# Mixture-of-experts network: the second expert stage scatters its rows to token order, and the last stage loads them as contiguous rows

## The reference

```
x = x + tanh(g_xattn[0]) * attention(norm(x), ctx)         # 16 heads of 64, a bias from side
x = x + tanh(g_ffn[0])   * experts(norm(x))                # 64 experts, best 4, silu, 256 rows each
x = x + tanh(g_xattn[1]) * attention(norm(x), norm(ctx))   # scores clipped to +-11
x = x + tanh(g_ffn[1])   * experts(norm(x))                # 8 experts, best 2, gelu, 1280 rows each
```

## Time and profile before

| | us |
|---|---|
| median of 3 runs | 2124.15 |
| the profiled execution | 2128.7 |
| its span, first to last instruction | 2127.0 |
| experts 1: first instruction to the last row copy's end | 1651.3 to 2035.6 |
| combine: barrier to the end of the span | 2038.0 to 2127.0 |

### The profile page before, as it was taken

How to read it: one execution, slowest core, us unless ns; L and a number is a source line. 1 busy time by engine, 2 the same in 40 slices (tenths; PEclk the granted TensorE clock), 3 DMA queues, 4 the chain that set the end, 5 groups by cost and what they waited for, 6 DMA issues and landing times. The chain is left out here.

```text
span 2127.0 us, 43848 instructions
## 1 busy us (share of the span) xinstructions
PE 1853.9 (87%) x14851; PEld 1671.5 (79%) x14851; DVE 1312.3 (62%) x3630; ACT 997.5 (47%) x2467; POOL 593.7 (28%) x712
## 2 busy tenths in 40 slices
PE   5999999999996599958999999999994699999920
PEld 4888888888885488847888888888883699999920
DVE  2677877877877233336778777878874444444423
ACT  3776677676674133334554454454551333333300
POOL 0012222222232200024243433434312422222056
PEclk9999999999998799978999999999997799999965
DMA  5676011011000599941111111111100422232134
GB/s 196 244 273 241 27 37 37 25 37 36 25 28 24 183 298 298 295 163 46 36 46 46 51 36 44 48 46 43 43 16 30 149 88 88 84 111 67 35 105 147
DMA packets 121821, 205.95 MB, mean 97 GB/s; under 512 B 15856, under 2 KB 63505, under 8 KB 121680
## 3 DMA queue, kind: packets, MB, share of 16 engines
q1 hardware_dynamic: 99408, 145.14, 20.1%
q0 software_dynamic: 22272, 59.05, 8.9%
HBM read 111.56 MB, written 94.37 MB: 97 GB/s over the span
## 5 line engine op out<-in xcount | busy, mean ns | idle before, releaser
L469 POOL DMA_INDIRECT buf<-a_rxn,a_disp x192 | 197.3, 1028 | 253.6 <-DVE comb L853 90.2
L1114 PE MATMUL a_psM<-a_wo,a_oT 128*128 128x256 f32 x1024 | 235.6, 383 | 4.5 <-ACT a_oT L621 1.4
L600 ACT ACTIVATE a_S<-a_S,a_mn 128x128 f32<-128x128 f32 x512 | 199.0, 396 | 68.8 <-DVE a_mn L889 68.8
L1114 PEld LDWEIGHTS a_psM<-a_wo,a_oT 128*128 128x128 f32 x1024 | 192.6, 191 | 36.0 <-issue 3.4
L79 PE MATMUL e_psH<-e_x_hi,e_w_hi 128*128 128x256 f32 x640 | 184.9, 289 | 0.0
L869 DVE TENSOR_TENSOR a_S<-a_S,a_rz 128x512 f32<-128x512 f32 x256 | 177.5, 693 | 8.8
L81 PE MATMUL e_psH<-e_x_hi,e_w_lo 128*128 128x256 f32 x640 | 181.7, 284 | 0.0
L80 PE MATMUL e_psH<-e_x_lo,e_w_hi 128*128 128x256 f32 x640 | 181.6, 284 | 0.0
L79 PE MATMUL a_psP<-a_c_hi,a_wk_hi 128*128 128x256 f32 x512 | 155.4, 303 | 11.1 <-DVE a_c_lo L746 11.1
L79 PE MATMUL a_psP<-a_x_hi,a_wq_hi 128*128 128x256 f32 x512 | 157.5, 308 | 5.2 <-DVE a_x_lo L746 5.2
L1077 PE MATMUL a_psT<-ident,a_S 128*128 128x128 f32 x1024 | 139.3, 275 | 18.7 <-DVE a_S L869 18.7
(11 more groups left out here) (184 smaller groups left out, 4904.6 us busy)
## 6 DMA issues: line engine op xcount, KB each, us to landing
y<-e_y SPq DMA_DIRECT2D x104, 256.0 KB, 2.9
buf<-a_zeros SPq DMA_DIRECT2D x16, 1280.0 KB, 7.0
buf<-a_zeros SPq DMA_DIRECT2D x16, 1024.0 KB, 5.9
e_rows<-buf SPq DMA_DIRECT2D x64, 256.0 KB, 3.9
e_w_in<-in_L_ffn_w SPq DMA_DIRECT2D x64, 256.0 KB, 3.2
a_ctx<-in_ctx SPq DMA_DIRECT2D x32, 256.0 KB, 2.9
e_w_out<-in_L_ffn_w SPq DMA_DIRECT2D x64, 128.0 KB, 3.8
e_w<-in_L_ffn_W_in SPq DMA_DIRECT2D x8, 1024.0 KB, 6.8
```

The lines of the kernel that those rows point to most:

```text
L469: g_.indirect_dma_start(out=buf, out_offset=bass.IndirectOffsetOnAxis(ap=disp[:, par, i, k:k + 1], axis=0), in_=rxn[:, par, i], in_offset= ...
L600: ins = a.activation(s[:, h], s[:, h], ACT.Exp, bias=mn[:, u % 2, h:h + 1], scale=-1.0, accum_out=z[:, u % 2, h:h + 1])
L1114: ins = mm(psM[:, 0], oT[:, c], wo[:, c], start=c == 0, stop=c == HP - 1)
```

## The change

Each row that attention 1 scatters to buf1 now carries its token's number plus one, in 8 added columns (rows of 264 numbers, 1056 bytes, instead of 256). Empty slots read zeros there. Experts 1 adds to this number, per chunk, a value for the slot (`target`): -1 for a first choice, 4095 for a second, 65535 for a slot past the expert's count. The sum is the row of y1, now 2 x 4096 rows in token order; rows past the bound are not written. GpSimd scatters each chunk by two indirect DMAs in place of SyncE's store, 7 chunks behind the gathers. `gates` moves to the end of VectorE's loop and no longer computes slots. y1 is cleared during attention 1 by 32 DMAs of 256 KB, since dropped choices are written by nobody. Combine loads y1 by 16 DMAs of 512 KB from SyncE into one tile for everything (4 token tiles and one choice each), and ScalarE issues the 16 stores. So that there are semaphores enough, those of attention 0 are cleared by GpSimd during experts 0, where it is otherwise idle.

The diff, cut to its core (semaphore renaming and tile allocations are left out):

```
@@ attention, SyncE
-                    for u in range(UG):
-                        sp.wait_ge(s_sc, at(g, WG, u // 2 + 1))
-                        clear(g * UG + u)
-                    load_ctx(g + 3)
+            sp.wait_ge(s_rwz, 2)
+            for g in range(PEEL):
+                for u in range(UG):
+                    sp.wait_ge(s_sc, at(g, WG, u // 2 + 1))
+                    n = g * UG + u
+                    if not first:
+                        clear("y1", s_zero[0], n, K1 * NTOK * D // P // 512 // (4 * UG), 512)
+                    elif n < 2 * UG:
+                        clear("buf0", s_zero[0], n, ROWS0 * D // P // 512 // (2 * UG), 512)
+                    else:
+                        clear("buf1", s_zero[1], n - 2 * UG, ROWS1 // P // (2 * UG), DW)
+                load_ctx(g + 3)
@@ attention, GpSimd
+                g_.memset(zeros[:], 0.0).then_inc(s_rwz, 1)
@@ attention, VectorE
+                if not first:
+                    ins = v_.tensor_copy(rxn[:, par, :, D:RW], tiles(t.token, g)...)
-                    v_.tensor_copy(tiles(t.idf1, g), idf[:])
@@ experts0
+        @block.gpsimd
+        def _(pool):
+            nc.clear_and_free_semaphores(t.done_sems)
@@ experts1, SyncE
-                    sp.wait_ge(s_ye, it * CB + c + 1)
-                    sp.dma_start(yd[...].rearrange("(p i) n -> p i n", p=P), y[:, c % 2]).then_inc(s_st[c % 2], 16)
@@ experts1, VectorE
+                v_.tensor_tensor(into[:, c % RB], rows[:, c % RB, :, D], target[...], ALU.add).then_inc(s_xlo, 1)
...
+                link(v_.tensor_scalar(source[:], source[:], -BIG, BIG - 1.0, ALU.mult, ALU.add))
+                link(v_.scalar_tensor_tensor(out=target[:], in0=second[:]..., scalar=float(NTOK),
+                                             in1=source[:]..., op0=ALU.mult, op1=ALU.add))
...
-            gates()
             for part in range(3):
                 ve.wait_ge(s_whi, part + 1)
                 weights_lo(0, part)
             each(ve, body)
+            gates()
@@ experts1, GpSimd
+            LAG = 7
+            def scatter(it, c):
+                pool.wait_ge(s_ye, it * CB + c + 1)
+                pool.sem_inc(t.s_passed, 1)
+                for i in range(GT):
+                    g_.indirect_dma_start(out=yd, out_offset=bass.IndirectOffsetOnAxis(ap=into[:, c % RB, i:i + 1], axis=0),
+                                          in_=y[:, c % 2, i], in_offset=None, bounds_check=K1 * NTOK - 1, oob_is_err=False
+                                          ).then_inc(s_st[c % 2], 16)
...
-                        pool.wait_ge(s_tx, (c if fresh else it * CB + c) - RB + 1)
+                        pool.wait_ge(s_xlo, (c if fresh else it * CB + c) - RB + 1)
...
+                    if not fresh or c >= LAG:
+                        scatter(*((it, c - LAG) if c >= LAG else (it - 1, CB + c - LAG)))
...
+            for c in range(CB - LAG, CB):
+                scatter(NIT - 1, c)
+            for i in range(2):
+                pool.wait_ge(s_st[i], NCH // 2 * (16 * GT))
@@ combine
-            for g in range(NG):
-                ...
-                for n in range(GT * K1):
-                    nc.gpsimd.indirect_dma_start(out=rows[:, g % 2, n], out_offset=None, in_=d["y1"], ...)
+            for q in range(NQ):
+                for k in range(K1):
+                    tiles = slice(q * QT, (q + 1) * QT)
+                    sp.dma_start(rows[:, k, tiles], src[k][:, tiles]).then_inc(s_row[q], 16)
...
+        @block.scalar
+        def _(act):
+            for g in range(NG):
+                q, i = divmod(g * GT, QT)
+                act.wait_ge(s_acc, QT * K1 * q + QT + i + GT)
+                nc.scalar.dma_start(d["out"][...], t.x[:, g * GT:(g + 1) * GT]).then_inc(s_out, 16)
```

More of the change, by code:

```diff
@@ new lines, in attention @@
+        s_tc = sem(L + "context_transposed")
+        NS = 3
+        s_xT = sem(L + "x_transposes_evacuated")
+        s_cT = sem(L + "context_transposes_evacuated")
+        s_pj = sem(L + "projected")
+        s_ev = [sem(L + f"projection_evacuated{i}") for i in range(2)]
+        s_sc = sem(L + "scores_ready")
+        s_read = sem(L + "scores_read")
+        s_exp = sem(L + "exp_ready")
+        RZ = 1 if first else 2
+        s_rz = sem(L + ("sums_inverted" if first else "sums_then_inverse_ready"))
@@ L243, in attention @@
             rows = m.sb(L + "rows", [P, GT * K0, D])
[L244 to L247, removed]
+            s_ix = sem(L + "indices_copied")
+            s_row = [sem(L + f"rows_gathered{i}") for i in range(2)]
+            s_acc = sem(L + "row_added")
+            s_cn = sem(L + "context_normed")
             cstats = m.sb(L + "cstats", [P, GT, 6])
@@ L251, in attention @@
             crs = m.sb(L + "crs", [P, GT])
-            s_cmv = m.sem(L + "context_stats_then_moments_ready")
-            s_cve = m.sem(L + "context_variance_shifted")
-            s_crs = m.sem(L + "context_rstd_ready")
-        else:
-            zeros = m.sb(L + "zeros", [P, 512])
-            s_min = m.sem(L + "min_ready")
-            s_zero = [m.sem(L + f"buffer_{i}_cleared") for i in range(2)]
+            s_cmv = sem(L + "context_stats_then_moments_ready")
+            s_cve = sem(L + "context_variance_shifted")
+            s_crs = sem(L + "context_rstd_ready")
+        else:
+            s_min = sem(L + "min_ready")
+        zeros = m.sb(L + "zeros", [P, 512])
+        s_zero = [sem(L + f"buffer_{i}_cleared") for i in range(2 if first else 1)]
         NR = 1 if first else 2
@@ L264, in attention @@
         rw = m.sb(L + "rw", [P, DC, EW])
-        rxn = m.sb(L + "rxn", [P, 2, GT, D])
+        RW = D if first else DW
+        rxn = m.sb(L + "rxn", [P, 2, GT, RW])
         rxT = m.sb(L + "rxT", [P, DC, TOK])
@@ L1413, in experts1 @@
         second = m.sb(L + "second", [P, E, NT])
+        moved = m.sb(L + "moved", [P, E, NT])
+        target = m.sb(L + "target", [P, E * NT])
+        into = m.sb(L + "into", [P, RB, GT], I32)
         source = m.sb(L + "source", [P, E, NT])
@@ L1442, in experts1 @@
         s_ye = m.sem(L + "output_evacuated")
-        s_st = [m.sem(L + f"rows_stored{i}") for i in range(2)]
+        s_st = [m.sem(L + f"rows_scattered{i}") for i in range(2)]
         block = stack.enter_context(nc.Block())
@@ L1497, in _ @@
             with sp.Fori(0, NIT - 1) as it:
[L1498 to L1501, removed]
+                body(it)
         RPI = CB // RB
@@ L1623, in split_x @@
                 ve.wait_ge(s_xhi, it * CB + c + 1)
-                v_.tensor_tensor(x_lo[:, c % 2], psX[c % 2][:], x_hi[:, c % 2].bitcast(F32), ALU.subtract
+                v_.tensor_tensor(x_lo[:, c % 2], psX[c % 2][:], x_hi[:, c % 2].bitcast(F32), ALU.subtract)
+                n0 = it * (CB * GT) + c * GT
+                v_.tensor_tensor(into[:, c % RB], rows[:, c % RB, :, D],
+                                 target[:, n0:n0 + GT] if isinstance(it, int) else target[:, bass.ds(n0, GT)], ALU.add
                                  ).then_inc(s_xlo, 1)
@@ L1773, in _ @@
-        @block.sync
-        def _(sp):
-            for g in range(NG):
-                sp.wait_ge(s_acc, GT * K1 * (g + 1))
-                sp.dma_start(d["out"][g * GT:(g + 1) * GT].rearrange("b p d -> p b d"), t.x[:, g * GT:(g + 1) * GT]
-                             ).then_inc(s_out, 16)
-            sp.wait_ge(s_out, 16 * NG)
+            for q in range(NQ):
+                ve.wait_ge(s_row[q], 16 * K1)
+                for k in range(K1):
+                    for i in range(QT):
+                        n = q * QT + i
+                        x = t.x[:, n]
+                        if k:
+                            ve.wait_ge(s_acc, QT * K1 * q + i + 1)
+                        nc.vector.scalar_tensor_tensor(out=x, in0=rows[:, k, n], scalar=t.prob1[:, n, k:k + 1],
+                                                       in1=x, op0=ALU.mult, op1=ALU.add).then_inc(s_acc, 1)
```

168 lines of the change are left out of this document (76 added, 92 removed).

## The result

The changed kernel takes 2071.28 us, the median of 4 runs (2070.71 to 2074.08), beside 2123.6 us of the kernel before on the same chip: a ratio of 0.9756 with a 95% interval from 0.9739 to 0.9773. It is 52 us faster, where 44 was forecast, and lies 0.3 us above the lower end of the range. The profiled execution took 2070.71 us, with a span of 2069.0.

What follows compares the result with a forecast made beforehand. It took TensorE to bound experts 1 and GpSimd's descriptor lists to bound combine. Combine saves 51 us, the seam costs 6.7, a gain of 44: from the median, 2124.15 - 44 = 2080 us, range 2071 to 2092.

Steps and rivals of the forecast that it cites:

- Combine, 38 us forecast: Last stage, from barrier to end: 38 us instead of 89.0, between 34.6 and 41.7, saving 51 us.
- the lower of the two bounds: Combine if loads never hold up VectorE: 4.9 first load + 26.7 adds + 2.6 last store + 0.4 barrier = 34.6 us.
- The sum of transfers: Combine's DMA: 22.8 us loads plus 12.1 us stores, 34.9 us; with latency and the end 37.3 us.
- The seam, 6.7 us forecast: Experts 1 to combine: last scatters, then GpSimd's drain of 6.0 us (3.0 to 9.0), open the barrier 6.7 us later.
- That it grows with the DMAs: Rival at the seam: the drain grows to 13.2 us with 160 DMAs, adding 7.2 us: 2087; chance 0.12.
- GpSimd in experts 1, 6.3 us per chunk forecast: Experts 1: a copy, two gathers and two scatters take GpSimd 6.3 of 9.06 us per chunk, hidden beside TensorE.
- the rival in which VectorE locks GpSimd out: Experts 1: GpSimd stands still through VectorE's work, 10.6 us per chunk, 61 us over 40 chunks: 2141; chance 0.02.
- The clearing in pieces of 1056 bytes: Attention 0: clearing costs by bytes, 59 us within 71, nothing lost; rival of double cost gives 2096, chance 0.06.
- TensorE still fills its window in experts 1 at 9.06 us per chunk: Sign of being right: experts 1 stays bound by TensorE at its earlier pace of 9.06 us per chunk.
- the prediction's own terms for its lower end: Whole kernel: combine at 34.6 instead of 38, drain at 3.0 instead of 6.0, and 2 us left open in attention 1.
- signs of being right: Barrier opens 2041 to 2048 after the drain; add gaps under 2 us, combine 35 to 42; experts 1 9.06 per chunk.
- the signs of being wrong: TensorE idle in experts 1 on x_lo or rows; drain over 10 us; adds waiting throughout combine; attention 0 ending later.

Runs made afterwards that it cites:

- the distance closed: Changed kernel with an unused 704-byte tile ahead of x_hi in experts 1, putting x and h back at the weights' address modulo 1024: 2079.13 us, ratio 0.9784.

## Why the prediction came out as it did

- **Combine, 38 us forecast, 34.2 measured.** The mechanism was right, and the lower of the two bounds (34.6, VectorE's path) was the better one. By pieces: the first add came 5.1 us behind the barrier (4.9 forecast), the adds took 25.42 (26.7 forecast), and 3.7 followed the last add (3.0 forecast). The sum of transfers was too long because they ran faster than the rates from which it was made. The DMA engines of the kernel after, from the barrier to the end, total and by queue:

```profile
DMA packets 6656, 12.58 MB, mean 360 GB/s; under 512 B 512, under 2 KB 4608, under 8 KB 6656
q1 hardware_dynamic: 2304, 8.39, 61.1%
q10 hardware_dynamic: 4352, 4.20, 34.1%
c_rows<-y SPq DMA_DIRECT2D x16, 512.0 KB, 10.1
```

  95% of 35 us for 12.58 MB are 378 GB/s while they run, against 368 and 348 taken from loads and stores apart. That is not a gain of running both at once: the loads alone, from 2038 to 2042 and ahead of the first store's data, moved 409 GB/s, and from 2050 to 2060 loads and stores together 410.
- **The seam, 6.7 us forecast, 7.5 measured.** The drain ended 6.7 us after the last scatter, the mean of four taken was 6.0. That it grows with the DMAs is refuted: 6.7 us after 160 DMAs in the stage, 6.6 after 80. It is 6.6 or 6.7 in all traces that keep the barrier, 2.9 and 8.9 or 9.0 in the attention stages: a fixed length for each place, whose cause stays open. Some 1.4 of the 6.7 us here are GpSimd's own wait for the scatters to land: the drain itself lasts 5.3 us, and where GpSimd does not wait first, in the run without the barrier, it ends 5.3 us after the last scatter.
- **GpSimd in experts 1, 6.3 us per chunk forecast.** Its timeline over one chunk, which answers to the earlier trace rows:

```profile
1881.37 1.01 POOL L1742 DMA_INDIRECT y<-e_y,e_into  x1 [2.17 <-DVE e_y L1663]
1882.69 1.00 POOL L1742 DMA_INDIRECT y<-e_y,e_into  x1 [0.30 <-issue]
1883.67 0.21 POOL L1753 COPY e_cur<-e_source_row 128x2 int32<-128x2 int32 x1
1884.71 1.01 POOL L1757 DMA_INDIRECT e_rows<-buf,e_cur  x1 [0.83 <-POOL e_cur L1753]
1886.03 0.96 POOL L1757 DMA_INDIRECT e_rows<-buf,e_cur  x1 [0.31 <-issue]
1890.20 1.01 POOL L1742 DMA_INDIRECT y<-e_y,e_into  x1 [3.21 <-DVE e_y L1663]
```

  5.6 us of work in 8.83, then a wait for a copy of the result: never the bound. The durations over the stage, scatters and gathers:

```profile
L1742 POOL DMA_INDIRECT y<-e_y,e_into x80: 971/1000/1019, 1687.4 to 2027.0; - x80
L1757 POOL DMA_INDIRECT e_rows<-buf,e_cur x80: 946/976/1930, 1653.9 to 1966.9; - x80
```

  No scatter took over 1.02 us, and the longest gather is as long as before, so the rival in which VectorE locks GpSimd out had no place here.
- **The clearing in pieces of 1056 bytes.** DMA from 122 to 193 us, which answers to the earlier trace rows:

```profile
q1 hardware_dynamic: 19435, 20.25, 87.4%
```

  20.25 MB in 87.4% of 71 us are 326 GB/s, against 365 with 2 KB pieces and some 188 if each piece had cost the same time. TensorE was busy 70.53 us of that stretch, 70.47 before. The size was a little off, and the cover held.
- **What failed: "TensorE still fills its window in experts 1 at 9.06 us per chunk".** It fills it, at 8.83 to 8.92. The prediction went through the instructions that the change adds and moves, and costed the wider rows as data only. That they also move the tiles behind them was visible in the edit, and its price, 8.4 us from first hidden product to last copy (365.3 with the distance closed, 356.9 without), could not be read from the rows of before, where all tiles stood at one distance. Without this effect the forecast of 2080 stands beside 2079.13; that it is so close owes something to chance, since combine saved 3.8 us more than forecast and the seam cost 0.8 more, while the profiled execution of before had been slower than the median. Luck also put the result inside the range: the prediction's own terms for its lower end give 2080 - 3.4 - 3.0 - 2 = 2071.6, which it rounded down to 2071, and 2071.28 was reached by an effect that is in none of them.
- **The signs that it named.** Three of its signs of being right did not come: the barrier opened at 2034.8, not between 2041 and 2048, because the last copy ended 10.8 us earlier than before; combine took less than 35 us; and a chunk took less than 9.06. The drain as the last thing before the barrier, the adds without gaps and the full window of TensorE did come, and none of the signs of being wrong.

The Trainium skill, SBUF — State Buffer, section SBUF: two separate sides, says that among the engines only the pair of ports shared by VectorE and GpSimd causes contention and that TensorE never waits on anyone. By that rule the place of TensorE's two operands would change nothing, and closing the distance would have left the kernel at 2071. It took 2079.13, at 120 ns between matmuls instead of 114 to 118; the measurement decides, for two tiles that one engine reads together, while no run here shows TensorE held up by another engine's reads.

## What to carry to other kernels

A change that resizes or drops a tile also moves every tile that is allocated after it; compare the number of matmuls in windows of equal length, not their busy share, before giving a difference to the edit itself. Where a stage is bound by TensorE, an unused tile of some hundred bytes between the operands that it reads together is a cheap thing to try; 320 bytes gave 8 to 10 us here, 256 and 512 gave nothing. And where GpSimd has issued indirect DMAs, put the wait for them on the engine that needs their data instead of a barrier: the barrier waits for GpSimd's drain as well, 5 us longer than the transfers.

## What the runs showed that was not expected

- Matmuls of 256 columns, in float32r (the type of these tiles), started every 119.8 to 120.0 ns in all four cases in which stationary and moving tiles were congruent modulo 256 bytes (at the same address but for a multiple of 256), and every 113.3 to 120.0 ns, as a mean over a chunk, at other distances, with a granted clock of 1.00 in each of the four windows shown.
- GpSimd's drain at the end of a block ended 2.9, 9.0 and 6.7 us after its last indirect DMA in three stages, the same to 0.1 us in all thirteen traces (eleven for the last, whose block two runs change).
- In the last stage loads alone moved 409 GB/s, and loads and stores together 410, over a few microseconds each; over the whole stage it was 378 while the engines ran.
